# TensorE's walk over the live chunks: nested tests of the remaining bits in place of a loop over all chunks

## What is computed

```python
q = (x @ W_q).reshape(b, n, HEADS, DIM_HEAD)
k = (context @ W_k).reshape(b, j, HEADS, DIM_HEAD)
v = (context @ W_v).reshape(b, j, HEADS, DIM_HEAD)
sim = jnp.einsum('bihd,bjhd->bhij', q, k) * scale
sim = jnp.where(mask[:, None, None, :], sim, max_neg)
attn = jax.nn.softmax(sim, axis=-1)
out = jnp.einsum('bhij,bjhd->bihd', attn, v).reshape(b, n, INNER)
return out @ W_o + b_o
```

## Time and profile before

| | us |
|---|---|
| median of 3 runs | 781.46 |
| lowest and highest | 776.91, 785.27 |
| profiled execution, device time | 780.1 |
| its span, first to last instruction | 778.4 |
| TensorE busy (matmuls) | 665.1 (85%) |
| VectorE busy | 442.5 (57%) |
| ScalarE busy | 356.1 (46%) |
| mean granted clock | 0.947 |

### The profile page before, as it was taken

How to read it: one execution, slowest core, us unless ns; L and a number is a source line. 1 busy time by engine, 2 the same in 40 slices (tenths; PEclk the granted TensorE clock), 3 DMA queues, 4 the chain that set the end, 5 groups by cost and what they waited for, 6 DMA issues and landing times.

```text
span 778.4 us, 14709 instructions
## 1 busy us (share of the span) xinstructions
PE 665.1 (85%) x4244; PEld 519.8 (67%) x4244; DVE 442.5 (57%) x960; ACT 356.1 (46%) x846; POOL 109.7 (14%) x143
## 2 busy tenths in 40 slices
PE   2896597969969696978969989999999899889996
PEld 1675486858858585867858867777777678634553
DVE  6822344444545444554475766666666534699974
ACT  2233233424434233433441136666666534468984
POOL 2581000010010101010020002222222100012211
PEclk9998888988989987998989999999999999999999
DMA  8000000000000000000545774444453243000111
GB/s 311 23 22 22 2 21 21 22 2 22 22 20 22 2 21 22 22 2 20 190 167 193 272 274 163 163 163 163 163 163 136 109 163 118 6 1 15 27 25 42
DMA packets 40064, 64.86 MB, mean 83 GB/s; under 512 B 4056, under 2 KB 20440, under 8 KB 40032
## 3 DMA queue, kind: packets, MB, share of 16 engines
q1 hardware_dynamic: 40032, 64.45, 24.3%
HBM read 53.95 MB, written 10.49 MB: 83 GB/s over the span
## 4 chain that ended last, share of the span: by engine, by line
PE 64%; DVE 13%; issue 11%; DMA 4%; DVEq 3%; ACT 2%; POOL 1%; SPq 0%; ACTq 0%; POOLq 0%
PE bank L570 33%; PE bank L699 6%; PE bank L930 5%; PE bank L687 3%; DMA absw<-in_L_ffn_w_down_dram 3%; PE bank L672 3%; PE bank L938 2%; PE bank L845 2%; PE bank L589 2%; DVE asum L1584 2%; DVE tern L1634 2%; DVE xn_a L1353 1%; PE bank L822 1%; PE bank L880 1%; PE bank L833 1%
## 5 line engine op out<-in xcount | busy, mean ns | idle before, releaser
L1049 ACT ACTIVATE probs<-probs,negm 128x256 f32<-128x256 f32 x104 | 52.1, 501 | 109.0 <-DVE negm L1450 109.0
L1450 DVE CUSTOM_DVE_ANT_0 probs<-bank,bias,negm_old 128x256 f32<-128x256 f32 x104 | 46.0, 480 | 64.2 <-PE bank L672 62.1
L672 PE MATMUL bank<-kT_hi,qT_hi 64*128 64x256 f32 x104 | 23.2, 440 | 51.6 <-issue 47.8
L930 PE MATMUL bank<-w_T,xqT 128*128 128x512 bf16 x256 | 58.4, 379 | 4.6 <-ACT xqT L1231 2.0
L467 POOL TENSOR_TENSOR rstd<-var_eps,neg_half 128x1 f32 (+1 forms) x16 | 10.0, 623 | 329.6 <-DVE var_eps L1513 260.3
L699 PEld LDWEIGHTS bank<-v_sb,pT 128*128 128x128 f32 x416 | 52.3, 191 | 5.5
L699 PE MATMUL bank<-v_sb,pT 128*128 128x64 f32 x416 | 54.7, 274 | 0.0
L1342 DVE TENSOR_TENSOR kT_lo<-bank,kT_hi 128x512 fp32r<-128x512 f32 x28 | 19.4, 692 | 58.2 <-ACT kT_hi L1038 58.2
L672 PEld LDWEIGHTS bank<-kT_hi,qT_hi 64*128 64x128 f32 x104 | 11.3, 214 | 61.3 <-issue 49.9
L1042 ACT COPY v_sb<-bank 128x512 f32<-128x512 f32 x28 | 15.1, 590 | 76.5 <-PE bank L699 73.5
L930 PEld LDWEIGHTS bank<-w_T,xqT 128*128 128x128 bf16 x256 | 24.1, 98 | 34.7 <-issue 2.9
(11 more groups left out here) (236 smaller groups left out, 1691.5 us busy)
## 6 DMA issues: line engine op xcount, KB each, us to landing
tern_dram<-tern SPq DMA_DIRECT2D x8, 768.0 KB, 5.2
tstage<-tern_dram SPq DMA_DIRECT2D x8, 768.0 KB, 4.3
cx<-in_ctx_dram SPq DMA_DIRECT2D x14, 384.0 KB, 2.9
absw<-in_L_ffn_w_gate_dram SPq DMA_DIRECT2D x8, 512.0 KB, 3.7
absw<-in_L_ffn_w_up_dram SPq DMA_DIRECT2D x8, 512.0 KB, 5.3
absw<-in_L_ffn_w_down_dram SPq DMA_DIRECT2D x8, 512.0 KB, 6.8
tern_raw<-in_L_ffn_w_gate_dram SPq DMA_DIRECT2D x8, 512.0 KB, 6.3
tern_raw<-in_L_ffn_w_up_dram SPq DMA_DIRECT2D x8, 512.0 KB, 7.2
```

What stands on the lines that cost most here:

```text
L672: last = mm(bank[3 + j][:, 0:CHUNK], part(qT, a)[o:o + DH, g, :], part(kT, c)[o:o + DH, g, :], start=(a == c), stop=(a == "lo"))
L930: last = mm(bank[3 + 2 * which + c % 2][:], xqT[:, u, k * P:(k + 1) * P], w_T[:, which, k, c * 512:c * 512 + 512], start=(k == 0), stop=(k ...
L1049: fn(probs[:, h, :], probs[:, h, :], ACT.Exp, bias=negm[:, h:h + 1], scale=-1.0, accum_out=csum[:, h:h + 1]).then_inc(p_done, 1)
L1450: nc.vector.tensor_tensor_reduce(probs[:, h, :], bank[3 + h % 2][:, 0:CHUNK], bias[:], -SCALE, negm_old[:, h:h + 1], ALU.add, ALU.min, neg ...
```

## The change

On TensorE only, the inner loop over the 8 chunks goes away. A batch's 8 bits are masked into a register `left`; if it is not 0, its lowest set bit is cleared (left AND (left - 1)), the body runs, and the same test stands again behind it, nested inside, 8 deep. So the program holds 8 copies of the body, a batch runs as many of them as it has live chunks, and behind the last of these one branch leads over the copies left. `words[0]` is shifted by 8 once per batch. The body itself, the order of its parts, all waits and the other engines' loops stay as they are.

```diff
+        def each_live(eng, words, flag, body):
+
+            left = eng.alloc_register("chunks_left")
+            eng.reg_alu(left, words[0], (1 << NC) - 1, ALU.bitwise_and)
+            eng.reg_alu(words[0], words[0], NC, ALU.logical_shift_right)
+
+            def nest(depth):
+                with eng.If_ne(left, 0):
+                    eng.reg_alu(flag, left, 1, ALU.subtract)
+                    eng.reg_alu(left, left, flag, ALU.bitwise_and)
+                    body()
+                    if depth > 1:
+                        nest(depth - 1)
+
+            nest(NC)
+
         UNITS = 2 * PAIRS
@@
             with pe.Fori(0, B) as b:
-                with pe.Fori(0, NC // UNROLL) as c:
-                    for u in range(UNROLL):
-                        with live(pe, words[0], flag):
-                            chunk(b, pe.snap(done))
-                            pe.reg_add(done, done, 1)
+                def live_chunk():
+                    chunk(b, pe.snap(done))
+                    pe.reg_add(done, done, 1)
+
+                each_live(pe, words, flag, live_chunk)
                 next_batch(pe, words, flag)
```

## The result

| | before | after |
|---|---|---|
| median, us | 780.91 (6 runs) | 793.37 (6 runs) |
| lowest, highest | 776.91, 785.27 | 791.13, 797.54 |
| ratio to before, 95% interval | | 1.0176 (1.0144 to 1.0208) |
| span of the profiled execution | 778.4 | 791.7 |
| mean granted clock | 0.947 | 0.934 |

The change costs 12.5 us by the medians (1.6%), 1.8% by the ratio. The forecast was 786.4, with a change of less than 1% as the likeliest outcome (0.58); the time lies inside the range of 777 to 797, at the place of the first rival (795.6), but not by the first rival's mechanism.

The account below looks back on a forecast made before the run. VectorE's own walk was taken to hold each batch's first maximum, hiding most of TensorE's 43 us. Terms -2.4 (walk), +7.3 (clock) and 0 (code) gave +4.9 us on 780.1, 785.0, forecast as a 786.4 median; range 777 to 797.

Parts of the forecast that it names:

- the first rival: TensorE's exit over the remaining copies fetches code in every batch: 9.2 us, 795.6 us with the clock's cost; chance 0.27.
- What bounds a batch's start: First maximum needs both VectorE's walk and TensorE's scores; of TensorE's 43 us walk only 2.4 us are gained.
- The clock's term: First chunk of each batch: TensorE's earlier start and later idling prolong the low clock, costing 7.3 us in all.
- The price list: First chunks: 17.58 us when never low, about 2.4 us of low clock free, then 0.46 us per further us low.
- The upper bound given, 8.7: Largest cost allowed for low clock in first chunks: 2.4 us instead of 2.0, a ninth more in the slope.
- The code's size: TensorE's jumps over unused copies: 0 us taken if fetched packets stay, 9.2 us as the other end.
- I take 0: TensorE's code packets are kept together; only the first exit pays and its wait is hidden, so 0 us.
- The likeliest case: Clock cost with kept code: -2.4 + 7.3 + 0 = +4.9 us, own range 782 to 791; chance 0.40.
- That the clock never falls: TensorE's early scores keep 2.4 GHz through each batch's first chunk: -8.2 us, 773.3 us; chance 0.05.
- the kernel is 20 us faster or more: Sign of error: if the maximum does not wait for VectorE's walk, up to 5 us a batch come free.

Follow-up runs that it names:

- The mirror image: Kernel before the change, with VectorE and ScalarE looping over the live count and TensorE keeping its walk: 777.55 us, ratio 0.995.
- the counted loops: Kernel before the change, with the walks of TensorE, ScalarE and VectorE replaced by a loop run once per live chunk: 741.62 us, ratio 0.9481.
- the two kernels of two copies: Changed kernel with 2 copies of the body instead of 8: 784.76 us; the same with a walk of six empty tests put in front: 778.9 us.
- the counted loops with the fill: Loops over the live count on TensorE, ScalarE and VectorE, plus small overwritten matmuls in TensorE's idle moments, against the kernel before: 731.47 us, ratio 0.9372.
- the kernel with the longer fill: Changed kernel with 2 copies instead of 8 and each batch's first scores computed nine times instead of once: 781.15 us, ratio 1.0012.

## Why the prediction was wrong, point by point

- **What bounds a batch's start**: right, in full. The first maximum follows VectorE's own last test by 0.5 us in every batch (183.9 to 184.41 in batch 3), the gain was 1.9 us in batch 0 where 2.07 was said, and of 43 us of walk nothing more came out. (The 0.37 us of batch 1 show with two copies, where its seam is 10.44 instead of 10.79 us; with eight the wait for code covers them.) The mirror image and the counted loops show both halves.
- **The clock's term**: right in its mechanism and about right in size, 7.3 us said, 8.0 in the trace, 5.9 between the two kernels of two copies. The price list holds beyond its range: at 0.81 to 0.84 (6.2 to 7.6 us low) the chunks take 19.37 to 19.91 us, and 17.58 + 0.46 x (7.6 - 2.4) is 19.97. The mean low time is 6.2 us; 5.9 was said for seven of the batches and 6.4 for the other. The upper bound given, 8.7, holds only one of its two allowances at a time; both together make about 10, which changes nothing here.
- **The code's size: the step that failed**. "I take 0" for packets kept together, and 9.2 us if displaced in each batch. It measured 7.8 us in the trace and 8.6 in the medians, and by neither of the two ways. The exits do not pay in each batch; only three branches and one place within project_output wait. The working covered the first exit, and even that not fully: the first branch of 3.3 us is hidden as said (84.8 + 3.3 is 88.1), but a second one stands right behind it, around project_output, into the next packet, and takes 2.6 us more, so turn_output starts at 91.30 and batch 1 is 2.5 us late. And it took the tail as there for good once fetched; the first exit behind two copies waits again, 3.8 us, and project_output is stopped a second time for 2.15 us, at a place where nothing hides it: 5.3 us. I had asked only whether packets are missed in every batch or never, and had priced a miss as one fetch; here each miss was followed by a second one in the next packet, and that is where most of the cost is, as the kernels with four and six copies show. Why the exit behind the third batch waits again stays open.
- **The chances.** The likeliest case combined a right clock term with this 0. With the measured 7.8 in its place the parts make -1.9 + 8.0 + 7.8 - 0.6 = +13.3 us in the profiled executions, +12.5 in the medians. That this is near the first rival's 795.6 is luck: its 9.2 us were one wait before each of seven batches, and the 7.8 stand before two. By the Trainium skill's rule on taken branches (Runtime: NRT & Kernel Launch, Instruction fetch mechanics) every exit and every jump back would have paid; the trace shows the cost of such a branch (3.3 to 3.8 us) but no wait in the last five batches, whose jumps span seven to ten packets by the estimate of 1.1 packets a body.
- **The rivals.** That the clock never falls was rightly held unlikely for this change; it is what the counted loops with the fill reach on purpose. The sign "the kernel is 20 us faster or more", should VectorE's walk not be the bound, did not come: it was the bound, and its removal with TensorE's brings 40.

## What to carry to other kernels

Where several engines run the same skipping loop side by side, taking it from one engine only moves the wait to the next: remove it from all of them or leave it. An engine that gets ready earlier and then stands idle can be worse off than one that arrives in time, if its clock falls when it idles; price the low clock in the stretch behind the gap, not in the gap. Far branches over copies of a large body can cost even when they wait only a few times: 3.3 to 3.8 us a wait here, 2.2 to 2.6 more where the next packet was missing too, 8 us in all. Price each by its place: of a wait at the exit alone 0.1 to 0.4 us came through behind the first batch and 1.2 to 2.7 behind the third. A loop whose bound is the number of live items needs neither copies nor a walk (here every batch has at least one live chunk, and the counted loops rely on it).

## What the hardware showed unexpectedly

- Six empty tests per batch in front of the work make the kernel 5.9 us faster (778.9 against 784.76).
- A low clock of up to 2.4 us at a chunk's beginning costs nothing: a chunk that is never low leaves TensorE 1.3 us idle (16.24 busy of 17.58), and one that is 2.4 us low uses that up (17.60 of 17.60). The place matters as well: low for about 3.5 us, a chunk takes 18.05 us when the stretch stands at its beginning and 18.6 to 19.1 in the kernel with the longer fill, where it falls inside.
- The exit behind the third batch waited 3.8 us, 80 us after the same target had been reached, though only one packet had come in between (at 160 us); in the remaining 235 us no branch waited again. The cause is open.
